# One chunk of the shared expert moved behind the block loop, and the work of the last stage redistributed between VectorE and GpSimd

## What is computed

```
x = layernorm(x + attention(x, w_qkv, w_out))
probs = softmax(x @ gate_w.T);  idx = top_k(probs + gate_b, 6)          # of 16 experts
for e in range(16):  y += cw[:, e] * ((silu(x @ w1[e].T + b1[e]) * (x @ w3[e].T + b3[e])) @ w2[e].T + b2[e])
z = (silu(x @ ws1.T + bs1) * (x @ ws3.T + bs3)) @ ws2.T + bs2            # the shared expert, 352 wide
out = layernorm(x + y + z)
```

## Time and profile before

| | us |
|---|---|
| median of 3 runs | 1139.32 |
| the runs | 1139.49, 1139.32, 1127.47 |
| the profiled execution, its own time | 1130.5 |
| its span, first to last instruction | 1128.7 |
| mean granted TensorE clock, share of full | 0.974 |

### The profile page before, as it was taken

The page is one execution under the profiler, slowest core; times in us unless marked ns, Lnnn a source line. Parts: engine busy times, 40 slices in busy tenths (PEclk is TensorE's granted clock), DMA queues, the critical chain, the costliest instruction groups (busy, mean ns, idle before and its releaser), DMA issues.

```text
span 1128.7 us, 28318 instructions
## 1 busy us (share of the span) xinstructions
PE 1036.1 (92%) x8028; PEld 847.3 (75%) x8029; DVE 748.7 (66%) x2401; ACT 670.9 (59%) x1680; POOL 740.6 (66%) x676
## 2 busy tenths in 40 slices
PE   7899998989898998788998999999999999999991
PEld 4546464646464644387988999999999999999991
DVE  8786878786878787577765555555555555555455
ACT  3567676767676765665555555555555555555544
POOL 4224368787878888877635666666666666666665
PEclk9999999999999998899998999999999999999996
DMA  6624254545454535557867666677776666667593
GB/s 185 183 71 114 77 143 147 164 147 163 148 161 145 169 124 172 189 174 228 287 165 139 115 120 119 114 118 117 119 118 113 110 116 113 116 116 140 82 313 144
DMA packets 127037, 163.54 MB, mean 145 GB/s; under 512 B 18800, under 2 KB 107504, under 8 KB 126704
## 3 DMA queue, kind: packets, MB, share of 16 engines
q1 hardware_dynamic: 82240, 99.73, 31.6%
q0 software_dynamic: 39024, 54.29, 25.6%
q10 hardware_dynamic: 5696, 8.55, 2.4%
HBM read 65.36 MB, written 73.85 MB: 123 GB/s over the span
## 4 chain that ended last, share of the span: by engine, by line
PE 63%; DMA 12%; DVE 12%; issue 5%; ACT 4%; POOL 2%; SPq 1%; ACTq 0%; POOLq 0%; DVEq 0%
PE psum L1057 13%; PE psum L794 10%; PE psum L1084 10%; DMA z_d<-y_sb,tokens 9%; PE psum L836 5%; PE psum L824 4%; PE psum L809 4%; DVE rowmax L1496 3%; PE psum L1042 3%; PE psum L1068 3%; PE psum L1053 3%; PE psum L1023 2%; ACT probs L1160 2%; DMA stack_q<-shift_l 2%; PE psum L811 2%
## 5 line engine op out<-in xcount | busy, mean ns | idle before, releaser
L1160 ACT ACTIVATE probs<-psum 128x512 f32<-128x512 f32 (+2 forms) x384 | 186.5, 530 | 115.1 <-PE psum L824 113.2
L1496 DVE TENSOR_REDUCE rowmax<-psum 128x1 f32<-128x512 f32 (+3 forms) x352 | 211.7, 632 | 60.5 <-PE psum L811 58.7
L2029 POOL DMA_INDIRECT xs_d<-x1p,index x192 | 206.1, 1074 | 53.2 <-issue 40.3
L2103 POOL DMA_INDIRECT x_d<-y_sb,tokens x104 | 162.5, 1562 | 93.6 <-ACT y_sb L1354 65.7
L2103 POOL DMA_INDIRECT z_d<-y_sb,tokens x103 | 160.7, 1560 | 93.7 <-ACT y_sb L1354 51.1
L1835 DVE TENSOR_TENSOR xb_lo<-psum,xb_hi 128x256 fp32r<-128x256 f32 x207 | 87.7, 424 | 201.3 <-ACT xb_hi L1151 199.4
L1057 PE MATMUL psum<-we_hi_lo,xb_hi 128*128 x828 | 200.9, 324 | 0.0
L1354 ACT ACTIVATE y_sb<-psum,combine 128x256 f32<-128x256 f32 x207 | 98.3, 475 | 152.2 <-PE psum L1084 75.2
L1084 PE MATMUL psum<-we_hi_lo,hb_hi 88*128 (+1 forms) x828 | 175.2, 304 | 0.0
L809 PE MATMUL psum<-stack_k,stack_q 96*128 96x256 bf16 (+3 forms) x512 | 139.0, 311 | 9.2 <-DVE rowmax L1496 3.6
L1057 PEld LDWEIGHTS psum<-we_hi_lo,xb_hi 128*128 128x128 f32 x828 | 146.8, 190 | 0.0
(11 more groups left out here) (209 smaller groups left out, 2322.3 us busy)
## 6 DMA issues: line engine op xcount, KB each, us to landing
xb<-xs_d SPq DMA_DIRECT2D x207, 138.0 KB
stack_q<-q_h SPq DMA_DIRECT2D x48, 128.0 KB
stack_k<-k_h SPq DMA_DIRECT2D x45, 128.0 KB
w_raw<-in_we SPq DMA_DIRECT2D x9, 608.0 KB, 4.2
xT_raw<-in_xT SPq DMA_DIRECT2D x9, 512.0 KB, 4.2
stack_q<-q_m SPq DMA_DIRECT2D x32, 128.0 KB
stack_k<-k_m SPq DMA_DIRECT2D x32, 128.0 KB
x_res<-in_x SPq DMA_DIRECT2D x8, 512.0 KB, 3.7
```

The costliest lines, as they stand in the source:

```text
L1160: nc.scalar.activation(probs[kt][:, heads[0]:heads[0] + n, :], st[f % ST_BANKS][:, 0:n * width].rearrange("p (h t) -> p h t", h=n), ACT.Ex ...
L1496: nc.vector.reduce_max(rowmax[gpar][:, heads[0]:heads[0] + n, qt], src, AX.X).then_inc(sm_free, 1)
L2029: nc.gpsimd.indirect_dma_start(out=xs_d[:, :], out_offset=bass.IndirectOffsetOnAxis(ap=index[tp][:, n:n + 1], axis=0), in_=x1p[tp][:, n // ...
L2103: nc.gpsimd.indirect_dma_start(out=(x1_d, z_d)[k % 2][:, :], out_offset=bass.IndirectOffsetOnAxis(ap=tokens[:, k:k + 1], axis=0), in_=y_sb ...
```

## The change

One chunk more lies behind the loop: 27 tiles ahead, 21 behind. In the tail DVE makes every low half, POOL makes every chunk's sum (three ahead), and chunk 9, the first one that PE finishes behind the loop, is finished first. DVE starts with the final chunks at T1 + 8 = 35. A sixteenth chunk needs a PSUM bank used before, so PE waits there for the first chunk's addition. In the front the last batch's later stages and the tables stand one or two tiles later, and the scatters and pads are paced faster.

```diff
-HC1 = 10
+HC1 = 9
-EPILOGUE_AT = {2: ("t0", "t1"), 4: ("p0", "p1"), 6: ("x0", "x1"), 8: ("r",), 10: ("d",)}
-NORMALIZE_TILE, SOFTMAX_TILE, STORE_X1_TILE, RANK_TILE = 5, 9, 8, 10
+EPILOGUE_AT = {2: ("t0", "t1"), 4: ("p0", "p1"), 7: ("x0", "x1"), 9: ("r",), 12: ("d",)}
+NORMALIZE_TILE, SOFTMAX_TILE, STORE_X1_TILE, RANK_TILE = 5, 10, 9, 12
-TABLE_TILES = (11, 12, 14)
+TABLE_TILES = (13, 14, 16)
-PACED_FROM, TILES_TO_SCATTERS = 9, (2, 3)
-PADS_FROM, TILES_TO_PADS = 13, (3, 4)
+PACED_FROM, TILES_TO_SCATTERS = 10, (1, 2)
+PADS_FROM, TILES_TO_PADS = 14, (1, 2)
-FINAL_FROM = DVE_LOW_UP_TO = T1 + 9
-SUMS_BY_POOL, NORMALIZED_BY_ACT = HC1 + 2, T_ALL // HT_TOK - 4
+FINAL_FROM, SUMS_AHEAD = T1 + 8, 3
+NORMALIZED_BY_ACT = T_ALL // HT_TOK - 4
+FINAL_ORDER = (HC1,) + tuple(i for i in range(T_ALL // HT_TOK) if i != HC1)
+SUM_BANKS = 6
 def sum_of(hc):
-    if hc < HC1 + 2:
-        return y_ps[(hc + (hc >= HC1)) % 2]
-    return (xt_ps + ht_ps)[hc - HC1 - 2]
+    if hc < HC1:
+        return y_ps[(hc + HC1) % 2]
+    return (y_ps[::-1] + xt_ps + ht_ps)[(hc - HC1) % SUM_BANKS]
 # PE, shared_down
+    elif t == 0 and hc >= HC1 + SUM_BANKS:
+        pe.wait_ge(z_done, hc - SUM_BANKS + 1)
 # DVE
-def final_add(i):
+def final_add(m):
+    i = FINAL_ORDER[m]
     dve.wait_ge(down_done, ST * (i + 1))
-    y = sum_of(i).rearrange("p (q d) -> p q d", q=HALF)
-    if i < SUMS_BY_POOL:
-        dve.wait_ge(fin_sum, i + 1)
-        nc.vector.tensor_tensor(fin_x[i][:], y, fin_x[i][:], ALU.add).then_inc(z_done, 1)
-    else:
-        dve.wait_ge(fin_loaded[i], 32)
-        nc.vector.tensor_tensor(fin_z[i][:], y, fin_z[i][:], ALU.add).then_inc(fin_y, 1)
+    dve.wait_ge(fin_sum, m + 1)
+    nc.vector.tensor_tensor(fin_x[i][:], sum_of(i).rearrange("p (q d) -> p q d", q=HALF), fin_x[i][:],
+                            ALU.add).then_inc(z_done, 1)
-def final_stats(i):
-    if i >= SUMS_BY_POOL:
-        dve.wait_ge(fin_y, i - SUMS_BY_POOL + 1)
-        nc.vector.tensor_tensor(fin_x[i][:], fin_x[i][:], fin_z[i][:], ALU.add).then_inc(z_done, 1)
...
 for T in range(T1 + 2, FINAL_FROM + HALVES):
     if T < T_SH:
         hide(T)
-    if T - 1 < DVE_LOW_UP_TO:
+    if T - 1 < T_SH:
         low(T - 1)
...
 # POOL
-for T in range(DVE_LOW_UP_TO, FINAL_FROM + HALVES):
-    i = T - FINAL_FROM
-    if i == 0:
-        final_sum(0)
-        final_sum(1)
-    if T < T_SH:
-        low(T)
+for m in range(SUMS_AHEAD):
+    final_sum(m)
+for m in range(HALVES):
     for k, (_, end) in enumerate(FINAL_GROUPS):
-        if i == end:
+        if m == end:
             final_inverse(k)
-    if i + 2 < SUMS_BY_POOL:
-        final_sum(i + 2)
+    if m + SUMS_AHEAD < HALVES:
+        final_sum(m + SUMS_AHEAD)
 final_inverse(len(FINAL_GROUPS) - 1)
```

More of the change, by code:

```diff
@@ L769, in _ @@
                 sp.wait_ge(added[n], 16 * ((BLOCKS + 1 - n) // 2))
[L770 removed]
+                for i in FINAL_ORDER[:FINAL_FIRST]:
                     load_final(i, src, dst)
[L772 removed]
+            for i in FINAL_ORDER[FINAL_FIRST:]:
                 load_final(i, x1_d, fin_x)
                 load_final(i, z_d, fin_z)
[L775 to L776 removed]
+            for m in range(HALVES):
+                store_final(m)
             sp.wait_ge(out_stored, 16 * HALVES)
@@ L1390, in blocks, with normalized @@
                         split_late_w(m, half)
-            def normalized(i):
-                act.wait_ge(fin_shift_done, [first <= i for first, _ in FINAL_GROUPS].count(True))
-                for q in range(HALF if i < NORMALIZED_BY_ACT else 1):
+            def normalized(m):
+                i = FINAL_ORDER[m]
+                act.wait_ge(fin_shift_done, [first <= m for first, _ in FINAL_GROUPS].count(True))
+                for q in range(HALF if m < NORMALIZED_BY_ACT else 1):
                     last = nc.scalar.activation(fin_x[i][:, q, :], fin_x[i][:, q, :], ACT.Identity,
-                                                bias=fin_shift[:, i, q:q + 1], scale=fin_rstd[:, i, q:q + 1])
+                                                bias=fin_shift[:, m, q:q + 1], scale=fin_rstd[:, m, q:q + 1])
                 last.then_inc(fin_done, 1)
@@ L1465, in _ @@
             high(T_SH - 1)
-            for i in range(T_SH - FINAL_FROM - NORMALIZED_BEHIND, HALVES):
-                normalized(i)
+            for m in range(T_SH - FINAL_FROM - NORMALIZED_BEHIND, HALVES):
+                normalized(m)
         @block.vector
@@ L1900, in final_stats, with final_aggregate, normalized_half @@
                 else:
-                    dve.wait_ge(fin_sum, i + 1)
+                    dve.wait_ge(fin_sum, m + 1)
                 for q in range(HALF):
-                    last = nc.vector.bn_stats(fin_stats[:, i, q, :], fin_x[i][:, q, :])
+                    last = nc.vector.bn_stats(fin_stats[:, m, q, :], fin_x[i][:, q, :])
                 last.then_inc(fin_stats_done, 1)
-            def normalized_half(i):
-                dve.wait_ge(fin_shift_done, [first <= i for first, _ in FINAL_GROUPS].count(True))
-                nc.vector.tensor_scalar(fin_x[i][:, 1, :], fin_x[i][:, 1, :], fin_rstd[:, i, 1:2], fin_shift[:, i, 1:2],
+            def final_aggregate(m):
+                dve.wait_ge(fin_stats_done, m + 1)
+                settle(dve, passed_dve)
+                for q in range(HALF):
+                    last = nc.vector.bn_aggr(fin_mv[:, m, q, :], fin_stats[:, m, q, :])
+                last.then_inc(fin_mv_done, 1)
+            def normalized_half(m):
+                i = FINAL_ORDER[m]
+                dve.wait_ge(fin_shift_done, [first <= m for first, _ in FINAL_GROUPS].count(True))
+                nc.vector.tensor_scalar(fin_x[i][:, 1, :], fin_x[i][:, 1, :], fin_rstd[:, m, 1:2], fin_shift[:, m, 1:2],
                                         ALU.mult, ALU.add).then_inc(fin_half_done, 1)
@@ L1951, in _ @@
                     low_x1(split_x1_of(T))
-                i = T - FINAL_FROM
-                if i >= HC1:
-                    final_add(i)
-                if i >= 1:
-                    final_aggregate(i - 1)
-                if i >= 0:
-                    final_stats(i)
+                m = T - FINAL_FROM
+                if m >= 0 and FINAL_ORDER[m] >= HC1:
+                    final_add(m)
+                if m >= 1:
+                    final_aggregate(m - 1)
+                if m >= 0:
+                    final_stats(m)
             final_aggregate(HALVES - 1)
-            for i in range(NORMALIZED_BY_ACT, HALVES):
-                normalized_half(i)
+            for m in range(NORMALIZED_BY_ACT, HALVES):
+                normalized_half(m)
         @block.gpsimd
```

42 lines of the change are left out of this document (15 added, 27 removed).

## The result

| | before | after |
|---|---|---|
| median of 19 runs each, us | 1133.65 (1126.17 to 1140.36) | 1129.12 (1120.30 to 1135.63) |
| ratio, 95% interval | | 0.9947 [0.9926, 0.9969] |
| span of the profiled execution, us | 1128.7 | 1124.3 |
| mean granted TensorE clock | 0.974 | 0.969 |

The account below looks back on a forecast made before the run. PE was taken to set the loop, carried over unchanged; the front's scatters and POOL's lateness in the tail left room. Front -2.8 and tail -5.5 gave -8.3 us, -0.73%, so a median of 1131.0 us, range 1116 to 1139.

Parts of the forecast that it names:

- the later path counts: Front: of PE's path (9.6 us earlier) and the scatters' path, the later sets the first block; gain 2.8 us.
- a first block later than 567: Front: sign in the changed profile that would make the front's step wrong.
- the term charged with 0.5 us: Front: PE's granted clock falls behind its wait of some 3 us for the first rows; 0.5 us lost.
- the first rival: Only the tail gains, the front being DMA-bound; change -5 us, 1134; chance 0.18.
- last down 3.6 us later: Tail: PE's last `down` ends near 1110.1 instead of 1106.5, with three more tiles and 4.0 us of POOL waits removed.
- charged 1.5 us: Tail: DVE's low halves meeting POOL's sums, 0.2 to 0.4 us each, 1.5 us in all; tail gain 5.5 instead of 7.0.
- the fourth rival: Tail: DVE waits out a POOL sum at each of 13 low halves; +2.8 us, or +5.6 without front gain, 1145; chance 0.08.
- the sign of a wrong tail step: Tail: PE waits for DVE's low halves of over 3 us in sum would make the tail's step wrong.
- From the last down to the end: Tail: three chunks left on DVE until 1113.9, POOL's last inverse until 1116.2, then 5.4 us to the end at 1121.7.
- under 8 us: Tail: more than 8 us from the last `down` to the last shift would make the tail's step wrong.
- The third rival: Tail gets no shorter, POOL's sums stretching to 1.75 us; total -4 to 0 us, 1137; chance 0.12.
- moved chunk: Three tiles fewer in front, 6.5 us off PE's path there, and three more behind the loop, +6.5 us.

Follow-up runs that it names:

- sums_cut: The changed kernel with each of POOL's 16 final sums cut to 8 of 256 columns, all loads and waits kept; ratio to before 0.9963 [0.9921, 1.0004].
- after_again: The changed kernel again, unchanged, on chip 1; ratio to the kernel before 1.0018 [0.9970, 1.0067].
- before_again: The kernel before the change, unchanged, profiled a second time on chip 2; 1163.36 us, ratio 1.0000 [0.9959, 1.0040].

## Why the prediction was right, and where its steps were not

**The result.** Forecast −0.73%, measured −0.53% with an interval from −0.74 to −0.31%; the time, 1129.12 us, lies in the range beside the forecast's 1131.0. That the two are so near is luck. The forecast stood on a median of three runs, 1139.32 us, which over 19 runs became 1133.65: 5.7 us too high a base, against a gain taken 3.8 us too large (8.3 for the 4.5 between the medians). The sum of its terms was too good by 5 us of stage time: the two stages gained 3.2 us, and what the whole gained beyond that, 1.2 us in the profiled pair and up to 2.8 by the ratio, lies where the change touches nothing. On chip 1 the gain couldn't be seen at all (1.0018 [0.9970, 1.0067]); that the changed kernel as it stands is faster rests on one measurement.

**Front, "the later path counts".** Right in its mechanism: the scatters' path set the loop's start, and PE's path gained 11.1 us (9.6 forecast) that were worth nothing. The size was off, −0.3 for −2.8, and by the prediction's own sign (a first block later than 567) the step is wrong: it came at 571.3, and at 567.9 if the 3.4 us by which the front began later are taken off. What is missing are 1.7 us at the landing, 0.3 us in the first load (2.5 us for 2.2) and 0.5 us of clock. The index came 4.2 us later, not 3.3; it was queued behind item 10's split, as forecast:

```profile
525.90 1.43 DVE L1486 TENSOR_TENSOR we_hi_lo<-w_raw,we_hi_lo 128x1216 fp32r<-128x1216 f32 x1 [0.78 <-ACT we_hi_lo L1155]
527.25 0.22 DVE L1638 TENSOR_TENSOR place<-psum,carry 128x64 f32<-128x64 f32 x1
...
528.39 0.18 DVE L1650 TENSOR_SCALAR index<-top_place 128x24 uint32<-128x24 f32 x1
```

```profile
529.38 1.34 POOL L2030 DMA_INDIRECT xs_d<-x1p,index  x1 [3.98 <-issue]
```

POOL, which had been idle for 3.98 us, issued its first scatter 0.8 us behind the index, for 0.2 in the sum. 23 steps then took (562.38 − 529.38) / 23 = 1.435 us each (1.42 forecast), and the landing came at 84.4 us where the forecast had 560.1 − 477.4 = 82.7. The clock was the term charged with 0.5 us. The wait was 10 us and not 3. The changed kernel's stretch from 560 to 568 (columns as above) shows the granted clock at 0.51, the mean of a stretch nearly all at the lower level, 1.2 GHz:

```profile
560.00:568.00 8.00, 0.16 (x1) 0.16 (x2) 1.05 (x3) 0.31 (x2) 3.68 (x7) 0.51 0.55 181
```

From the first transposition of rows to the first block's start PE then took 3.47 us (567.84 to 571.31), for 2.46 before (565.74 to 568.20, the matmul ahead of the one in the earlier trace rows): 1.0 us lost, 0.5 charged. The clock stood at 0.50 until 573.5 and at 1.00 from 574 on, so that the loop's first 2.5 us ran at the lower level too; the prediction had no term for that, and the loop's own spread hides it. Behind these stands an error of another kind: the sum let scatters issued earlier land earlier. In the runs none landed before 83.5 us, however early they were issued, which is the mechanism of the first rival. Had the landing come between 83.5 and 84.8, as in the other kernels, the row load would have left at most 2.5 us earlier than before (83.6 for 86.2), and with the 1.3 us that load and clock took back the front would have gained at most 1.2 us, not 2.8.

**Tail, "last down 3.6 us later".** It came 7.3 later (54.9 for 47.6). Without meetings, in `sums_cut`, it came 3.6 later (51.2), as sliding PE's tail by three tiles and removing the 4.0 us had given; but `sums_cut` ran on chip 2, where the last `down` of before came at 49.3, so that the agreement to a tenth is chance. What was mis-sized is the meeting of low halves with sums: charged 1.5 us, measured 3.7 on the last `down` and, with POOL's part, 4.6 on the tail (4.6 and 4.9 between two kernels on chip 2). The row near which the charge was taken, the low half at 1081.03 with 0.63 us, was a late start and no price of a meeting: the sum that began at 1080.08 had 0.35 us left, and 0.22 us were added to 0.41, the same rule as in the changed kernel. Of the changed kernel's low halves six were clearly stretched (0.78, 1.54, 1.16, 1.14, 1.10, 1.00), by 4.3 us in all, and two `low_x1`, by 2.1 us, which the forecast hadn't counted among them. Only those that begin within a sum pay, and then by what is left of it, less 0.12 to 0.15 us. Over the forecast's 13 low halves 4.3 us are 0.33 each, within its 0.2 to 0.4, which is luck where a single row stood behind it; the error lies in what it set against that, some 0.4 us of slack per tile, and in leaving out `low_x1`. The 0.75 from which the change would have lost were not reached: the fourth rival's mechanism, at part of its price. PE's waits for DVE's low halves, 2.8 us, lie just under the 3 us that the prediction had named as the sign of a wrong tail step.

**From the last down to the end.** Forecast 6.1 us to the last shift; 6.6 measured (1112.3 to 1118.9), 16.8 before. (The forecast's own sum is 0.4 us too long: 1109.2 + 3 x 1.39 + 0.3 is 1113.7, not 1113.9, and 2.1 more is 1115.8, not 1116.2.) Of the signs this one held, under 8 us. DVE had three chunks left, as forecast, and stood 0.68 us for POOL's last sum, which came at 1114.63 and not at 1112.2:

```profile
1114.75 0.69 DVE L1886 TENSOR_TENSOR fin_x<-psum,fin_x 128x512 f32<-128x512 f32 x1 [0.68 <-POOL fin_x L2109]
```

**The third rival**, POOL's sums stretched to 1.75 us, didn't come: fours took 5.42 us, 1.36 each, once 5.93. The stretched engine is DVE, not POOL, wherever POOL began first; in the group of 5.93 us two sums took 1.54 and 1.74 us, each beside a DVE operation that had come first.

**What the step "moved chunk" was worth.** The forecast summed the tail as one piece. Taken apart, by stages, the new division gained 7 to 8 us and the chunk moved behind the loop cost 2.6 to 4.6, against 1.3 to 2.2 us in front: with whole sums the move was a loss of some 2 us, too small for any pair of timed kernels here to show. With halved sums it cost the tail nothing (64.9 and 64.6 us with seven chunks, 65.4 and 64.5 with six).

## What to carry to other kernels

Before work is taken from an engine at a meeting point of several paths, work out all paths to it, DMA engines included: 11 us saved on PE bought 0.3 us. A single meeting of DVE and POOL in a trace is no price for a dense stretch; look how much of the partner's instruction was left when it began, take that rest at each start that falls inside one, and count every operation with two SBUF inputs, not only the one that is moved. Shorter instructions on POOL help only while POOL has pauses to pay for them.

## What the runs showed of the hardware

DVE operations with two SBUF inputs waited out POOL's current sum (0.41 to 1.54, 0.69 to 1.78 us), at a price of what was left of it less 0.12 to 0.15 us; those with one input in PSUM did not (0.66 to 0.69 us throughout). A sum that began second waited likewise (1.54 and 1.74 us for 1.30). The rule as such was weighed ahead; that nearly a whole sum is waited out, 1.13 us at the worst, the trace of before did not show, whose low half met only the last 0.35 us of a sum.

The time differs between chips by more than the change is worth, in the front and in the attention. On chips 1 and 2 ACT stood still before a `silu` for up to 11.3 us, for something that the profile calls `remote`, no engine or queue of this core; in the attention of these profiles its waits of this kind come to 15 to 24 us. ACT's waits in the front and its timeline in `after_again`:

```profile
ACT hidden L1319 <- remote: 20.6, 3, 11.1
```

```profile
518.77 0.41 ACT L1155 ACTIVATE h_hi<-hidden 128x256 fp32r<-128x256 f32 x1
525.59 0.47 ACT L1319 ACTIVATE hidden<-psum,bias 128x256 f32<-128x256 f32 x1 [6.41 <-remote]
```

and in `before_again`:

```profile
ACT hidden L1315 <- remote: 8.5, 3, 3.8
```

Such waits of ACT, 7.6 to 20.6 us in sum, stand in the fronts of all eight profiles of chips 1 and 2 and in none of the six others. What ACT waited for isn't settled by any run.
